# Fetching the sums of a graph's nodes group by group, before the last slot is stored

## The chip, the cores and the metric

The kernel runs on one core of a Trainium2 chip. The metric is the device time of one execution in microseconds. Three executions of the kernel before took 3168.97, 3172.85 and 3183.3 us; their median is 3172.85 us. A change is told by the median of the new kernel beside that of the old one.

## The reference

There are 6250 nodes with 64 features and 200,000 edges, sorted by their target node `dst`. Two graph networks follow each other:

```python
h = relu(layernorm(x))
# network 0: three layers of log-sum-exp over the neighbours
h = h @ W_in.T + b_in
for l in range(3):
    agg = log(segment_sum(exp(h[src]), dst))
    h = 0.5 * h + 0.5 * relu(layernorm(concat(h, agg) @ W_l[l].T + b_l[l]))
x = x + h
# network 1: a message per edge, summed per node, then a gated update
m = silu(silu(concat(x[src], sh, radial) @ W1 + b1) @ W2 + b2) @ W3 + b3
agg = segment_sum(m, dst)
u_in = concat(x, agg)
gate = sigmoid(u_in @ G + gb)
u = silu(layernorm(u_in @ U1 + ub1))
out = x + gate * layernorm(u @ U2 + ub2)
```

The sum over edges is linear in `W3` and `b3`, so the kernel sums first and multiplies by `W3` afterwards; the bias then comes in as `b3` times the node's number of edges (its degree).

## The kernel before

The nodes lie in J = 49 columns of 128. The kernel has these stages.

**Setup and counts.** VectorE makes two masks over the edges and SP stores them in device memory (L428 to L432). A flag (`way_known`) then chooses a way; with these inputs it is `by_counts`. There TensorE makes, from one-hot matrices, a matrix of edge counts between nodes, one block per column (L810), and multiplies it at once by the first layer's exponentials (L791). ScalarE copies each block out of PSUM in eleven pieces (`fill_block`, L1194) into one of two buffers, and SP stores the block (L474). `fill_block` of block j waits until block j - 2 is stored. Layers 2 and 3 read the blocks back. At the end of the counting `last_edges` computes, for each node, the row of its last edge (`end_idx`), in a dozen small operations on 128x49 elements.

**Messages.** The edges are cut into 391 slots of 512 (NSLOT). For each slot GpSimd gathers the rows of the source nodes with four indirect DMAs of 128 rows (L663), into a ring of 15 slots; every fifteenth slot is picked by matrix products instead (L961). TensorE transposes the rows (L950), multiplies by W1 (L973) and W2 (L980), with ScalarE's silu after each. VectorE scans along the slot (L2118) with a mask that restarts the sum at each new target node, so the scan at a node's last edge holds its whole sum. Four slots later TensorE multiplies the scan by W3 (`rows_back`, L988) into one PSUM bank, ScalarE copies it out (`rows_out`, L1342), and SP stores it as 512 rows of 64 numbers into `scan_rows` in device memory (`store_rows_of`, L550; in `sp.dma_start(scan_rows[bass.ds(s * BE, BE), :]...)`). One further row of `scan_rows`, number NO_EDGES, is zero and stands for nodes without edges. Five output buffers (OUT_RING) are used in turn, so that `rows_out` of slot s waits until slot s - 5 is stored.

**The end.** GpSimd waits until all slots are stored, and then fetches for each of the 49 columns the rows of its nodes' last edges with an indirect DMA that adds to `ybuf` (L678). `ybuf` holds b3 times the degree from a product on VectorE (L2131). The columns are in nine groups (END_GROUPS: seven of 6, one of 4 and one of 3). TensorE first multiplies 32 and then 8 filler products (`keep_busy`, L1027), whose results nobody reads. For each group: TensorE transposes the sums (`turn_agg`, L1037), ScalarE copies them (L1401), TensorE multiplies by U1 and G (`update_in`, L1049), VectorE adds the bias (L2153), ScalarE squares, VectorE reduces (L2176), ScalarE takes the root (L1388), VectorE scales (L2192), TensorE transposes (L1059), ScalarE applies silu (L1409), TensorE multiplies by U2 (`update_out`, L1068), and VectorE adds, normalises (L2198 to L2200) and applies the gate (`let_through`, L2206). GpSimd adds the result to x (L683) and SP stores it (L578). All engines run this as a pipeline, in which group i's first half stands beside the second halves of groups i - 1 to i - 3; the order is written out by hand and each engine keeps it.

**What sets the order.** Each engine works through its own list, with semaphores between. SP queues the mask stores, then the count blocks, then the loads and stores of the slots and of the output, all on one queue. GpSimd issues only the indirect DMAs and, at the end, the residual additions. `turn_done` counts the turned slots plus 15, so GpSimd's wait for `LOOP * i + k + 1` holds until the ring's slot is free.

Of the kernel before, what the change touches and what calls it, by code (L numbers as in the profile page):

```python
# [8 lines left out]
I32 = mybir.dt.int32  # L9
# [6 lines left out]
P = 128  # L16
# [23 lines left out]
LAG = 4  # L40
IDX_STEP = 5
# [71 lines left out]
def build(nc, x_in, dst_in, prev_in, first_in, src_in, src_row, rows_in, attr_in, w_in, v_in, out):  # L113
    with ExitStack() as ctx:
# [33 lines left out]
        end_idx = sb("end_idx", [P, J], I32)  # L148
# [109 lines left out]
        m_back = [ps[:, 2 + TERM_RING, k * TB * D:(k + 1) * TB * D] for k in range(BACK_RING)]  # L258

# [138 lines left out]
        update_ready, hT_stored, hT_loaded, let_in = (sem(n) for n in ("update_ready", "hT_stored", "hT_loaded", "let_in"))  # L398
# [15 lines left out]
        def _(sp):  # L414
# [17 lines left out]
            sp.wait_ge(masks_stored, 6 * DMA)  # L432

# [130 lines left out]

            for k in range(LOOP):
                move_slot(k, k)
# [7 lines left out]
            for s in range(NSLOT - LAG, NSLOT):  # L574
                store_rows_of(s, s % OUT_RING)
            for i, (a, n) in enumerate(END_GROUPS):
# [6 lines left out]
        def _(pool):  # L583
# [90 lines left out]
            for k in range(OUT_RING):  # L674
                pool.wait_ge(e1.stored[k], DMA * ((NSLOT - k + OUT_RING - 1) // OUT_RING))
            for i, (a, n) in enumerate(END_GROUPS):
                for j in range(a, a + n):
                    pool.indirect_dma_start(ybuf[:, j, :], None, scan_rows,  # L678
                                            bass.IndirectOffsetOnAxis(ap=end_idx[:, j:j + 1].bitcast(U32), axis=0),
                                            compute_op=ALU.add).then_inc(rows_fetched[i], DMA)  # L680
            for i, (a, n) in enumerate(END_GROUPS):
                pool.wait_ge(let_in, i + 1)
                pool.tensor_tensor(xres[:, a:a + n, :], xres[:, a:a + n, :], ybuf[:, a:a + n, :], ALU.add).then_inc(y_ready, 1)  # L683
# [3 lines left out]
        def _(pe):  # L687
# [294 lines left out]
            def rows_back(s, k, late):  # L982

                pe.wait_ge(e1.scan_done, s + 1)
                if late:
                    pe.wait_ge(e1.out_ready, s - BACK_RING + 1)
                for t in range(TB):
                    last = pe.matmul(m_back[k % BACK_RING][:, t * D:(t + 1) * D], m_scan[:, k % SCAN_RING, t * P:(t + 1) * P], W("W3"),  # L988
# [30 lines left out]
            for s in range(NSLOT - LAG, NSLOT):  # L1019
                rows_back(s, s % LOOP, True)  # L1020
# [8 lines left out]
            def turn_agg(i, a, n):  # L1029
# [5 lines left out]
                pe.wait_ge(rows_fetched[i], FETCHED + n * DMA)  # L1035
# [35 lines left out]
            keep_busy(6, 32)  # L1071
# [14 lines left out]
        def _(act):  # L1086
# [250 lines left out]
            def rows_out(s, k, lap):  # L1337
# [946 lines left out]
```

## Time and profile before

| | |
|---|---|
| median of three executions | 3172.85 us |
| profiled execution | 3195.68 us, span 3194.0 us |
| mean granted TensorE clock | 0.925 |
| TensorE, products / weight loads | 86% / 68% |
| VectorE | 60% |
| ScalarE | 51% |
| GpSimd | 47% |

Shares are of the span. The profile was taken from one execution; its time stands beside its span because what comes from the profile has to be put on its time. A busy TensorE is not TensorE at its peak, and a group's mean duration mixes both of its clock levels. In the lines of the profile L663 is line 663 of the kernel, PE is TensorE, DVE VectorE, ACT ScalarE, POOL GpSimd and SPq SyncE's queue of DMA issues. "Issue" is time in which the engine waited for nothing that the profile shows.

### The profile page before, as it was taken

How to read it: one execution, taken by the hardware profiler on the slowest of the kernel's cores; microseconds unless marked ns; L12 is line 12 of the kernel's file. 1: busy time of each engine (PE TensorE's matmuls, PEld its weight loads, DVE VectorE, ACT ScalarE, POOL GpSimd, SP SyncE). 2: the span in 40 equal slices, each digit the busy share in tenths (PEclk: the TensorE clock that was granted, in tenths of full speed). 3: DMA queues.
4: the chain of work that ended last, by engine and by line, in shares of the span. 5: the costliest groups of instructions: out<-in, count | busy, mean ns of one | idle time of the engine just before them, and what ended most of it. 6: DMA issues, size and time to landing. Idle time of an engine off the chain costs nothing.

```text
span 3194.0 us, 63519 instructions
## 1 busy us (share of the span) xinstructions
PE 2752.0 (86%) x20761; PEld 2179.8 (68%) x20761; DVE 1919.2 (60%) x2346; ACT 1613.8 (51%) x2994; POOL 1515.6 (47%) x1572
## 2 busy tenths in 40 slices
PE   4499999967999985889888989888989898898975
PEld 3377777757998982666666666666767666676654
DVE  5899999964444564455555555555555555555526
ACT  2488888832332223455545555545555554555534
POOL 4000000000000006777777777777777777777765
PEclk9999999968999996899999999999999999999976
DMA  3133333326998973445444445544445555444421
GB/s 109 61 141 161 141 161 141 161 121 260 365 361 320 359 287 79 107 121 132 120 119 119 122 117 125 129 121 121 121 117 125 119 128 124 120 121 116 126 48 30
DMA packets 216659, 477.09 MB, mean 149 GB/s; under 512 B 53932, under 2 KB 114910, under 8 KB 197601
## 3 DMA queue, kind: packets, MB, share of 16 engines
q1 hardware_dynamic: 159976, 422.33, 38.5%
q0 software_dynamic: 55632, 52.47, 10.3%
q10 hardware_dynamic: 1001, 1.66, 0.1%
q8 instruction: 28, 0.46, 0.1%
q14 instruction: 22, 0.18, 0.0%
HBM read 339.87 MB, written 136.41 MB: 149 GB/s over the span
## 4 chain that ended last, share of the span: by engine, by line
PE 47%; POOL 25%; issue 11%; DVE 11%; DMA 4%; ACT 1%; DVEq 0%; POOLq 0%; ACTq 0%
POOL arena L663 22%; PE ps L791 14%; PE ps L961 8%; PE ps L810 6%; PE ps L973 5%; PE ps L980 5%; PE ps L988 5%; DMA arena<-m_tab,m_idx 3%; DVE arena L1868 2%; POOL ybuf L678 2%; PE ps L950 2%; DVE stageT L1844 2%; PE ps L706 1%; PE ps L694 1%; POOL arena L604 0%
## 5 line engine op out<-in xcount | busy, mean ns | idle before, releaser
L663 POOL DMA_INDIRECT arena<-m_tab,m_idx x1463 | 1391.4, 951 | 1586.0 <-issue 1574.8
L2118 DVE TENSOR_TENSOR_SCAN arena<-arena,ps 128x512 f32<-128x512 f32 x391 | 500.2, 1279 | 856.6 <-ACT ps L1335 723.4
L988 PEld LDWEIGHTS ps<-weights,arena 128*128 128x128 f32 x3128 | 438.2, 203 | 210.3 <-issue 196.4
L1330 ACT ACTIVATE arena<-ps,weights 128x512 f32<-128x512 f32 x391 | 268.7, 687 | 490.7 <-PE ps L973 483.1
L791 PE MATMUL ps<-arena 128*128 128x195 bf16 (+1 forms) x4802 | 481.5, 248 | 32.2 <-DVE arena L1810 31.6
L791 PEld LDWEIGHTS ps<-arena 128*128 128x128 f16 x4802 | 416.8, 98 | 62.8 <-DVE arena L1810 31.8
L961 PE MATMUL ps<-ends,arena 128*128 128x192 bf16 x4900 | 458.9, 252 | 0.0
L973 PE MATMUL ps<-arena,weights 81*128 81x512 f32 x782 | 443.5, 651 | 0.0
L980 PE MATMUL ps<-arena,weights 128*128 128x512 f32 x782 | 435.9, 640 | 0.0
L961 PEld LDWEIGHTS ps<-ends,arena 128*128 128x128 bf16 x4900 | 421.7, 100 | 7.0
L988 PE MATMUL ps<-weights,arena 128*128 128x64 f32 x3128 | 415.4, 279 | 1.7 <-ACT arena L1342 1.7
L1323 ACT ACTIVATE arena<-ps 64x256 f32<-64x256 f32 x782 | 293.9, 376 | 218.5 <-PE ps L950 210.9
L1194 ACT ACTIVATE arena<-ps 128x588 f16<-128x588 f32 (+1 forms) x539 | 346.7, 644 | 107.0 <-PE ps L810 97.5
L2099 DVE TENSOR_SCALAR arena<-stage,node_no 128x3096 bf16<-128x3096 int16 (+1 forms) x225 | 368.9, 1640 | 0.0
L1868 DVE TENSOR_TENSOR arena<-arena 128x2352 bf16<-128x2352 f16 (+1 forms) x294 | 351.3, 1223 | 16.6 <-PE ps L810 16.6
L950 PE MATMUL ps<-ident,arena 128*128 128x128 f32 x782 | 165.5, 296 | 207.8 <-DMA arena<-m_tab,m_idx 204.6
L1335 ACT ACTIVATE ps<-ps,weights 128x512 f32<-128x512 f32 x391 | 258.8, 662 | 96.8 <-PE ps L980 93.5
L980 PEld LDWEIGHTS ps<-arena,weights 128*128 128x128 f32 x782 | 160.1, 205 | 207.9 <-issue 207.2
L950 PEld LDWEIGHTS ps<-ident,arena 128*128 128x128 f32 x782 | 97.2, 167 | 228.1 <-issue 224.9
L810 PE MATMUL ps<-arena 128*128 128x294 bf16 x1078 | 192.8, 298 | 34.2 <-DVE arena L1868 30.8
L791 PE MATMUL ps<-wide,arena 128*128 128x192 bf16 x2401 | 204.8, 247 | 6.4 <-DMA arena<-count_d 3.6
L791 PEld LDWEIGHTS ps<-wide,arena 128*128 128x128 f16 x2401 | 200.7, 99 | 7.2 <-issue 3.7
(269 smaller groups left out, 2294.1 us busy)
## 6 DMA issues: line engine op xcount, KB each, us to landing
arena<-count_d SPq DMA_DIRECT2D x98, 1568.0 KB, 8.5
arena<-keep_d SPq DMA_DIRECT2D x391, 256.0 KB, 3.9
count_d<-arena SPq DMA_DIRECT2D x49, 1568.0 KB, 5.1
scan_rows<-arena SPq DMA_DIRECT2D x391, 128.0 KB
arena<-m_tab,m_idx POOLq DMA_INDIRECT x1463, 3.3
arena<-attr_in SPq DMA_DIRECT2D x391, 34.0 KB
arena<-src_row SPq DMA_DIRECT2D x25, 258.0 KB
hT_d<-stageT ACTq DMA_DIRECT2D x12, 132.0 KB
```

Of the source, the lines that this page charges most:

```text
L663: pool.indirect_dma_start(m_rows[:, k, t, :], None, m_tab, bass.IndirectOffsetOnAxis(ap=m_idx[:, k, t:t + 1].bitcast(U32), axis=0))\
L791: last = pe.matmul(ps[:, bank, 0:rhs.shape[2]], blocks[block][:, a, :], rhs[:, a, :], start=(a == 0), stop=(a == J - 1), skip_group_check= ...
L810: last = pe.matmul(ps[:, bank, 0:WCOLS], hot_b[b][:, k % BATCH, :, i], hot_a[:, slot, k % UNIT, :, i], start=(i == 0), stop=(i == WT - 1))
L950: last = pe.transpose(m_turn[:, t // 2 * P:(t // 2 + 1) * P], m_rows[:, k, t:t + 2, :].rearrange("p t f -> p (t f)"), ident[:, :])
L961: last = pe.matmul(ps[:, 3 + TERM_RING + t // 2, (t % 2) * PARTS * D:(t % 2 + 1) * PARTS * D], pick[:, n % PICK_RING, (a - first) * PICK_C ...
L973: pe.matmul(m_in, W("W1"), m_msg[:, k % ATTR_RING, :], start=True, stop=True).then_inc(e1.in_done, 1)
L980: pe.matmul(m_term[k % TERM_RING], W("W2"), m_hid[:, k % HID_RING, :], start=True, stop=True).then_inc(e1.w2_done, 1)
L988: last = pe.matmul(m_back[k % BACK_RING][:, t * D:(t + 1) * D], m_scan[:, k % SCAN_RING, t * P:(t + 1) * P], W("W3"), start=True, stop=True)
L1194: act.activation(blocks[r][:, :, 2 * m * WD:2 * m * WD + 2 * wd].rearrange("p a (w d) -> p a w d", w=2), ps[:, two:two + 2, 0:wd * J].rear ...
L1868: dve.tensor_tensor(hot_a[:, u % HOT_SLOTS, 0:n, :, :], iota_w[:, :, :].unsqueeze(1).to_broadcast([P, n, WCOLS, WT]), keys, ALU.is_equal). ...
L2099: dve.tensor_scalar(of, src, node_no[:, first:first + 1], None, ALU.is_equal).then_inc(pick_ready, 1)
L2118: dve.tensor_tensor_scan(m_scan[:, k % SCAN_RING, :], m_mask[:, k % MASK_RING, :], m_term[k % TERM_RING], before, ALU.mult, ALU.add).then_ ...
```

## The change

1. The fetches at the end are plain ones instead of adding ones. Those of a group are issued as soon as the slots up to its last node's last edge are stored. VectorE computes that number for every node (`slots_needed`, four more operations in `last_edges`), GpSimd loads it into a register and waits for `out_ready` to reach it plus 5. After the last store SP adds 5 to `out_ready`, so that the last group's wait can end. A wait for `turn_done` keeps the semaphores of the gathers, which the fetches share, apart.
2. b3 times the degree goes to `hbuf` on VectorE, and VectorE adds it to each group's sums (`add_b3`), for group i + 1 ahead of group i's bias. TensorE waits for that.
3. VectorE adds the result to x, in place of GpSimd.
4. The last four slots' W3 products go to three PSUM banks in turn (`last_back`); the filler products move from bank 6 to bank 0.
5. SP stores zeros into the last 20 slots' rows of `scan_rows` (CLEARED), behind the masks, from the 64 zeros in one partition, and waits for it ahead of the first slot.

```diff
+CLEARED = LOOP + OUT_RING
+        last_back = [ps[:, 2 + TERM_RING + k % 3, 0:TB * D] for k in range(LAG)]
 @@ SP
             sp.wait_ge(masks_stored, 6 * DMA)
+            sp.dma_start(scan_rows[(NSLOT - CLEARED) * BE:NSLOT * BE, :], zero_row[:, :].unsqueeze(1).to_broadcast([1, CLEARED * BE, D]))\
+              .then_inc(zero_stored, DMA)
...
+            sp.wait_ge(zero_stored, 2 * DMA)
             for k in range(LOOP):
                 move_slot(k, k)
...
+            for k in range(OUT_RING):
+                sp.wait_ge(e1.stored[k], DMA * ((NSLOT - k + OUT_RING - 1) // OUT_RING))
+            sp.sem_inc(e1.out_ready, OUT_RING)
 @@ GpSimd
-            for k in range(OUT_RING):
-                pool.wait_ge(e1.stored[k], DMA * ((NSLOT - k + OUT_RING - 1) // OUT_RING))
             for i, (a, n) in enumerate(END_GROUPS):
+                needed = slots_needed[P - 1:P, a + n - 1:a + n]
+                pool.wait_ge(e1.turn_done, LOOP * (LAPS - 1) + i + 2)
+                pool.wait_ge(e1.out_ready, pool.to_reg(pool.value_load(needed, min_val=OUT_RING + 1, max_val=NSLOT + OUT_RING)))
+                pool.sem_inc(alone, 1)
                 for j in range(a, a + n):
                     pool.indirect_dma_start(ybuf[:, j, :], None, scan_rows,
-                                            bass.IndirectOffsetOnAxis(ap=end_idx[:, j:j + 1].bitcast(U32), axis=0),
-                                            compute_op=ALU.add).then_inc(rows_fetched[i], DMA)
-            for i, (a, n) in enumerate(END_GROUPS):
-                pool.wait_ge(let_in, i + 1)
-                pool.tensor_tensor(xres[:, a:a + n, :], xres[:, a:a + n, :], ybuf[:, a:a + n, :], ALU.add).then_inc(y_ready, 1)
+                                            bass.IndirectOffsetOnAxis(ap=end_idx[:, j:j + 1].bitcast(U32), axis=0))\
+                        .then_inc(rows_fetched[i], DMA)
 @@ TensorE
-            def rows_back(s, k, late):
+            def rows_back(s, k, late, to=m_back[0], ring=BACK_RING):
                 pe.wait_ge(e1.scan_done, s + 1)
                 if late:
-                    pe.wait_ge(e1.out_ready, s - BACK_RING + 1)
+                    pe.wait_ge(e1.out_ready, s - ring + 1)
...
-            for s in range(NSLOT - LAG, NSLOT):
-                rows_back(s, s % LOOP, True)
+            for n, s in enumerate(range(NSLOT - LAG, NSLOT)):
+                rows_back(s, s % LOOP, True, last_back[n], n + 1 if n < 3 else 3)
...
-                pe.wait_ge(rows_fetched[i], FETCHED + n * DMA)
+                pe.wait_ge(agg_ready, i + 1)
...
-            keep_busy(6, 32)
+            keep_busy(0, 32)
 @@ VectorE, last_edges
+                link(dve.tensor_scalar(mean[:, :], end_f[:, :], BE - 1.0, float(BE), ALU.add, ALU.max))
+                link(dve.tensor_copy(slots_needed[:, :], mean[:, :]))
+                link(dve.tensor_scalar(slots_needed[:, :], slots_needed[:, :], BE.bit_length() - 1, None, ALU.logical_shift_right))
+                link(dve.tensor_scalar(slots_needed[:, :], slots_needed[:, :], OUT_RING, None, ALU.add))
 @@ VectorE, the end
-                    link(dve.tensor_tensor(ybuf[:, :, :], per_node(deg_one[:, :, 0], D), per_feature(V("b3"), J), ALU.mult))
+                    link(dve.tensor_tensor(hbuf[:, :, :], per_node(deg_one[:, :, 0], D), per_feature(V("b3"), J), ALU.mult))
...
+            def add_b3(i, a, n):
+                dve.wait_ge(rows_fetched[i], FETCHED + n * DMA)
+                dve.tensor_tensor(ybuf[:, a:a + n, :], ybuf[:, a:a + n, :], hbuf[:, a:a + n, :], ALU.add).then_inc(agg_ready, 1)
...
-                dve.scalar_tensor_tensor(v, of_rows[:, a:a + n, HID:ROW], 1.0, v, ALU.add, ALU.mult).then_inc(let_in, 1)
+                link(dve.scalar_tensor_tensor(v, of_rows[:, a:a + n, HID:ROW], 1.0, v, ALU.add, ALU.mult))
+                dve.tensor_tensor(xres[:, a:a + n, :], xres[:, a:a + n, :], v, ALU.add).then_inc(y_ready, 1)
             for i, (a, n) in enumerate(END_GROUPS):
                 v = i - 2 if i >= 2 else None
+                if i == 0:
+                    add_b3(i, a, n)
+                if i + 1 < len(END_GROUPS):
+                    add_b3(i + 1, *END_GROUPS[i + 1])
                 add_update_bias(i, a, n)
```

ScalarE's `rows_out` reads the bank that `rows_back` wrote.

## Rows read from the trace of the kernel before

**Rows 1.** The page's chain that ended last, share of the span by line.

```profile
POOL arena L663 22%; PE ps L791 14%; PE ps L961 8%; PE ps L810 6%; PE ps L973 5%; PE ps L980 5%; PE ps L988 5%; DMA arena<-m_tab,m_idx 3%; DVE arena L1868 2%; POOL ybuf L678 2%; PE ps L950 2%; DVE stageT L1844 2%; PE ps L706 1%; PE ps L694 1%; POOL arena L604 0%
```

**Rows 2.** One line's instructions: count, duration in ns min/median/max, first and last start.

```profile
L663 POOL DMA_INDIRECT arena<-m_tab,m_idx x1463: 940/945/4143, 1207.0 to 3043.0; - x183
...
L678 POOL DMA_INDIRECT ybuf<-scan_rows,end_idx x49: 1531/1541/1936, 3063.7 to 3153.9; - x49
```

**Rows 3.** Timeline (start us, us, engine, line, operation, count), end of the message pass.

```profile
3042.99 0.95 POOL L663 DMA_INDIRECT arena<-m_tab,m_idx  x1 [0.30 <-issue]
...
3053.84 2.69 DVE L2118 TENSOR_TENSOR_SCAN arena<-arena,ps 128x512 f32<-128x512 f32 x2 [1.39 <-ACT ps L1335]
3053.94 1.00 PE L988 MATMUL ps<-weights,arena 128*128 128x64 f32 x8
...
3057.14 1.72 PE L988 MATMUL ps<-weights,arena 128*128 128x64 f32 x8 [0.57 <-ACT arena L1342]
...
3059.43 1.94 PE L988 MATMUL ps<-weights,arena 128*128 128x64 f32 x8 [0.56 <-ACT arena L1342]
...
3061.16 6.03 PE L1027 MATMUL ps<-ones 128*128 128x256 bf16 x40
...
3063.75 1.58 POOL L678 DMA_INDIRECT ybuf<-scan_rows,end_idx  x1 [19.81 <-DMA scan_rows<-arena]
```

**Rows 4.** Timeline of the end: groups 0 and 8, one group's products and transposes.

```profile
3077.74 0.80 ACT L1401 ACTIVATE wide<-ps 64x768 f32<-64x768 f32 x1 [15.95 <-PE ps L1037]
...
3078.69 4.18 PE L1049 MATMUL ps<-weights,wide 128*128 128x192 f32 x12 [0.98 <-ACT wide L1401]
...
3082.91 1.36 DVE L2153 TENSOR_TENSOR arena<-ps,rowvec 128x1152 f32<-128x1152 f32 x1 [26.37 <-PE ps L1049]
...
3098.79 1.46 PE L1037 MATMUL ps<-ident,ybuf 128*64 128x128 f32 x6 [4.36 <-DMA ybuf<-scan_rows,end_idx]
...
3122.35 2.66 PE L1068 MATMUL ps<-weights,stageT 128*128 128x64 f32 x12
...
3170.85 0.54 DVE L2153 TENSOR_TENSOR arena<-ps,rowvec 128x384 f32<-128x384 f32 x1
...
3185.85 0.59 POOL L683 TENSOR_TENSOR xres<-xres,ybuf 128x192 f32<-128x192 f32 x1 [1.47 <-DVE ybuf L2206]
```

**Rows 5.** Windows: start:end, length, busy us per engine, TensorE clock, DMA share, GB/s.

```profile
3070.00:3080.00 10.00, 2.80 (x10) 2.23 (x11) 0.00 (x0) 0.80 (x1) 8.48 (x6) 0.55 0.20 17
3106.03:3114.94 8.91, 4.72 (x36) 4.22 (x34) 4.99 (x9) 5.87 (x9) 7.39 (x6) 1.00 0.21 18
3129.00:3139.86 10.86, 8.19 (x38) 7.78 (x37) 7.23 (x13) 6.33 (x9) 9.23 (x6) 0.68 0.21 18
```

**Rows 6.** Timeline of VectorE at the end: an addition, and a small operation beside L683.

```profile
3116.79 0.56 DVE L2199 TENSOR_TENSOR ybuf<-ybuf,rowvec 128x384 f32<-128x384 f32 x1
...
3155.60 3.15 DVE L2172 TENSOR_SCALAR mean<-mean 128x6 f32<-128x6 f32 x1
```

**Rows 7.** Timeline: one operation on 128x49 in the last edges.

```profile
669.24 0.19 DVE L1636 TENSOR_SCALAR end_f<-end_f 128x49 f32<-128x49 f32 x1
```

**Rows 8.** Windows of the kernel's start, around the mask stores.

```profile
82.00:84.00 2.00, 0.19 (x1) 0.20 (x2) 1.83 (x7) 0.00 (x0) 0.00 (x0) 1.00 1.06 440
85.00:143.40 58.40, 19.77 (x88) 12.30 (x89) 51.47 (x77) 24.78 (x41) 0.00 (x0) 1.00 0.00 1
```

**Rows 9.** First count blocks: DMA issues, SP's timeline, ScalarE's timeline.

```profile
count_d<-arena SPq DMA_DIRECT2D x49, 1568.0 KB, 5.1
...
143.45 43.67 SPq L474 DMA_DIRECT2D count_d<-arena  x5
...
154.25 1.96 ACT L1194 ACTIVATE arena<-ps 128x392 f16<-128x392 f32 x3 [0.39 <-PE ps L810]
```

**Rows 10.** The page's DMA queues: packets, MB, share of 16 engines.

```profile
q1 hardware_dynamic: 159976, 422.33, 38.5%
q0 software_dynamic: 55632, 52.47, 10.3%
```

More of the change, by code:

```diff
@@ L147, in build @@
             "mean", "var", "rstd", "end_tile", "end_f", "start_f", "has", "degree"))
-        end_idx = sb("end_idx", [P, J], I32)
+        end_idx, slots_needed = sb("end_idx", [P, J], I32), sb("slots_needed", [P, J], I32)
         stage = sb("stage", [P, 2, GT, P])
@@ L397, in late_block @@
             return first % RING, first // RING + k + 1, first + RING * k
-        update_ready, hT_stored, hT_loaded, let_in = (sem(n) for n in ("update_ready", "hT_stored", "hT_loaded", "let_in"))
+        update_ready, hT_stored, hT_loaded, agg_ready = (sem(n) for n in ("update_ready", "hT_stored", "hT_loaded", "agg_ready"))
         agg_turned, agg_copied, agg_multiplied = (sem(n) for n in ("agg_turned", "agg_copied", "agg_multiplied"))
@@ L980, in hidden_out @@
                 pe.matmul(m_term[k % TERM_RING], W("W2"), m_hid[:, k % HID_RING, :], start=True, stop=True).then_inc(e1.w2_done, 1)
-            def rows_back(s, k, late):
+            def rows_back(s, k, late, to=m_back[0], ring=BACK_RING):
                 pe.wait_ge(e1.scan_done, s + 1)
                 if late:
-                    pe.wait_ge(e1.out_ready, s - BACK_RING + 1)
+                    pe.wait_ge(e1.out_ready, s - ring + 1)
                 for t in range(TB):
-                    last = pe.matmul(m_back[k % BACK_RING][:, t * D:(t + 1) * D], m_scan[:, k % SCAN_RING, t * P:(t + 1) * P], W("W3"),
+                    last = pe.matmul(to[:, t * D:(t + 1) * D], m_scan[:, k % SCAN_RING, t * P:(t + 1) * P], W("W3"),
                                      start=True, stop=True)
@@ L1335, in second_silu, with rows_out @@
                 act.activation(m_term[k % TERM_RING], m_term[k % TERM_RING], ACT.Silu, bias=W("b2")).then_inc(e1.silu2_done, 1)
-            def rows_out(s, k, lap):
+            def rows_out(s, k, lap, of=m_back[0]):
                 act.wait_ge(e1.back_done, s + 1)
@@ L1341, in rows_out @@
                     act.wait_ge(e1.stored[k % OUT_RING], DMA * ((LOOP // OUT_RING) * lap + k // OUT_RING))
-                act.activation(m_out[:, k % OUT_RING, :, :].rearrange("p t f -> p (t f)"), m_back[k % BACK_RING], ACT.Copy)\
+                act.activation(m_out[:, k % OUT_RING, :, :].rearrange("p t f -> p (t f)"), of, ACT.Copy)\
                    .then_inc(e1.out_ready, 1)
@@ L1368, in _ @@
                 second_silu(s, s % LOOP)
-            for s in range(NSLOT - LAG, NSLOT):
-                rows_out(s, s % LOOP, s // LOOP)
+            for n, s in enumerate(range(NSLOT - LAG, NSLOT)):
+                rows_out(s, s % LOOP, s // LOOP, last_back[n])
             def square_u(i, a, n):
```

## The prediction

> **What bounds the kernel now.** I read the chain of waits first, by line, and then in order of time. Its shares [rows 1] name two stretches that the change touches: the gathers of the message pass (L663) and the fetches at the end (L678). From 3000 us on, the chain is GpSimd's gathers, one after another, 1.25 us apart (0.95 us and 0.30 us of issue [rows 3]). The last gather is issued at 3043.0 [rows 2], so GpSimd reaches the end of its loop at 3044 and not fifteen slots early. It then waits 19.8 us for the last stored slot and issues 49 fetches, 1.84 us apart, from 3063.75 to 3155.5 [rows 2, 3].
>
> The timeline of the end shows the update of the nodes running in step with the fetches: VectorE adds the update bias (L2153) to group 0 at 3082.91, to group 8 at 3170.85 [rows 4]. A full group takes 10.9 us, as long as its six fetches (6 x 1.84 = 11.0). In that time VectorE is busy for 7.2 us and TensorE for 8.2 [rows 5]. The fetches are the bound, and after them the chain VectorE, ScalarE, TensorE. The profiled execution took 3195.68 us with a span of 3194.0, some 23 us above the median of 3172.85. I work out differences in the span and put them on the median.
>
> **The end, part by part.** *The last W3 products.* Four slots' products run from 3053.94 to 3061.37 [rows 3], each after the first waiting for ScalarE's copy out of the one bank (idle 0.57 us), the last two at a fallen clock (1.72 and 1.94 us instead of 1.00). With three banks only the scans hold them. The last two scans end at 3055.1 and 3056.5, so slot 390's product ends near 3058.3. That is 3 us gained.
>
> *The fetches.* A plain fetch has the shape of the gathers (128 rows of 256 B), so I price it like them at 1.25 us from one to the next. Bounds: 1.25 and 1.84, the accumulating form. GpSimd starts at 3044.3, since the turns that it now waits for (slots 377 to 385) are over by then, and so are the stores that groups 0 to 7 need (group 7 ends near slot 368: 5888 nodes x 32 edges / 512). Each group adds a register load and three waits, for which no row stands; 0 to 1 us each, I take 0.5. Group 0 is then in at 3044.3 + 8.0 + 3.3 = 3055.6, group 1 at 3064, group 8 (3 columns, after the last store at about 3061) at 3044.3 + 61 + 5 + 3.3 = 3114. The old wait of 19.8 us and the fetches no longer bound anything; late next is the chain of the updates.
>
> *The start.* TensorE goes from 3058.3 into its 40 filler products, now on the path. They took 6.0 us when they hid in the wait [rows 3]; at the full clock, which unbroken work should hold, some 4.5. Then transposes 0.8 to 1.5, copy 0.8, the products of group 0 2.1 to 4.2 (the rows' 1.46 and 4.18 are at the low level, and half of it at full clock) [rows 4] and 0.6 of hand-over: the first L2153 comes at 3068 (3067 to 3071) instead of 3082.91.
>
> *The groups.* VectorE's 7.23 us in a full group [rows 5] grow by adding b3 times degree and by the residual add, each a 128x384 float32 addition like L2199, 0.56 us [rows 6]: 8.35 of work. With the waits for square and square root between them I get 8.9. From the other side, TensorE at its low level needs 4.18 for L1049, 1.46 for each of two sets of transposes and 2.66 for L1068 [rows 4], 9.8 us per group and 10.1 with waits. The clock was 0.68 in one old group and 1.00 in another [rows 5], so I take 9.4. GpSimd's residual adds go, and with them stalls such as VectorE's 3.15 us at L2172, an operation on 128x6 elements, while L683 ran [rows 6]. From group 0 to 8: 8.7 + 6 x 9.4 + 7.8 = 72.9, so group 8's L2153 comes at 3141 instead of 3170.85. From there to the end were 23.15 us. VectorE's own adds replace GpSimd's 0.59 us last one [rows 4], but those of groups 5 to 7 stand ahead of it: 23.5.
>
> The end: 3141 + 23.5 = 3164.5, against 3194.0: 29.5 us gained. Bounds: 34 (periods of 8.9) and 20 (periods of 10.1, a late start, fetches at 1.84, by which group 8 would be in at 3044.3 + 90 + 5 + 3 = 3142, about 5 us late).
>
> **The start of the kernel.** Four small operations on 128x49 join the chain of the last edges, 0.19 us and the hand-over each [rows 7]: 0.9 us lost, on VectorE's path. The b3 product (3.4 us) is the same into another buffer.
>
> *The clearing transfer.* SP queues one store of 20 x 512 = 10,240 rows of 256 B, 2.62 MB, all read from one row of one partition. It starts when the masks have landed: the transfer engines stand from 85 on [rows 8], so the first bytes move at about 86. Up to 143.45 the DMA engines have nothing else to do [rows 8]. That is the cover, and it is limited: at 143.45 SP queues the first count block (1568 KB, 5.1 us to landing) on the same queue [rows 9], and ScalarE may fill the third block, whose buffer is that of the first, only when this one has landed. ScalarE begins it at 155.0, right behind the second (L1194, [rows 9]). So a clearing of up to 155.0 - 5.1 - 86 = 64 us is free. Every further microsecond delays the count stage, which is on the chain itself (L791 is 14% of it, L810 6% [rows 1]).
>
> No row shows a large store out of one partition; the other rows that bear on it spread over 128 partitions or go from HBM. From below: at 440 GB/s [rows 8] it takes 6 us, no loss. By the mean time of SP's packets, 38.5% x 16 x 3194 / 159,976 = 0.123 us [rows 10], 640 on each of 16 engines take 79 us. That is 15 us too long. By one partition's share: 440 GB/s over 16 engines is 27.5 GB/s for each, each with eight partitions of its own; if all sixteen must draw on one partition and get no more than one of them had, 2.62 MB take 95 us. From above: if rows out of one partition went one after another at an engine's own time for such rows (10.3% x 16 x 3194 us for some 197,000 rows [rows 2, 10] = 26.7 ns), 273 us.
>
> I take 95 us, since reading from a single partition is what sets this store apart. It ends at 181, the first count block lands at 186.4, and ScalarE waits from 155.0: 31.4 us. TensorE can work some 2 us ahead into its free banks. Against that, its clock will have fallen while it stood: after the idle 3063 to 3076 it read 0.55 from 3070 to 3080 [rows 5]. I leave the loss at 31.5.
>
> The Trainium skill (SBUF — State Buffer, "Door 1: the DMA port swizzle") says that four neighbouring partitions share one of 16 ports and reached 27.6 GB/s together. By it the clearing would take 95 us, and this trace has no such store to set against it. Another rule speaks against the change more strongly (DMA: Bandwidth & Descriptors, "Why small descriptors are slow"): a 256 B descriptor pays 3 cycles on top of 8. If that held at the port too, my estimate from these pages is 131 us, and the kernel would lose some 38 us net.
>
> **Sum.** -29.5 at the end, +0.9 in the last edges, +31.5 in the count stage: +3 us. On the median: 3176 us, no change. About 0.5% (16 us) is what a measurement of this kernel can tell from none.
>
> **Rivals.** *The clearing hides (faster).* If it is over in 64 us, only the gain is left: 3172.85 - 29.5 + 0.9 = 3144 us. For it speaks that 57 us of idle transfer engines lie ahead of the first block [rows 8]; against it that 2.62 MB come from one partition. Clearing by packets (79 us) would lie between: +13, 3157. Chance of a result under 3157: 0.30.
>
> *The clearing is slower than one engine's share (slower).* The sixteen engines' reads of one partition would get in each other's way. The place is the same wait of ScalarE for the third block. It decides from a clearing of 111 us on, where the net loss passes 16 us. At 273 us the wait would be 209 us: 3172.85 - 28.6 + 209 = 3353. Against it: no packet in the trace comes near such a cost; for it: no row excludes it. Chance of over 3189: 0.20.
>
> *The end gains less.* If a plain fetch also costs 1.84 us, or TensorE stays at its low level, the gain is 20 to 24 us. With the clearing at 95 us the time is 3182 to 3186, still no change; it only shifts within the cases. That the fetches don't start early at all would need GpSimd's new wait to hold until the last store at 3061; then 49 x 1.25 start there, group 0 is in at 3072 and the end gains about 13 us: 3192. One in twenty, inside the 0.20.
>
> **Numbers.** No change 0.50, faster 0.30, slower 0.20. The forecast is 3176; its own range 3166 to 3188. The range for 8 in 10 goes from 3139 (clearing hidden, periods short) to 3212 (a clearing 36 us longer than forecast), which cuts the slower case in half.
>
> **What would show it.** The clearing's time to landing, 95 us. L1194 idle for some 31 us before the third block near 155, and every later stage up to the last gather later by about 32 us. The last L988 product to the first L2153: 10 us. L2153 of full groups 8.9 to 10.1 us apart; L678 at 0.95 us; no POOL L683. I am wrong if the clearing lands before 150 (then faster), or if the L678 lines still run past 3120 of the old time scale.

## The result, and the profile after

The changed kernel takes 3170.1 us (median of 20 runs) against 3184.7 for the kernel before in the same rounds: a ratio of 0.9954 [0.9936, 0.9972], 14.6 us faster. The forecast was +3 us, no change. The forecast's base, 3172.85 us, was the median of three executions; the 20 give 3184.7. The executions of each kernel fall into two clusters, at 3171.0 and 3191.9 us before and at 3156.0 and 3170.9 after (their medians, with the executions taken beside a0; 15.0 and 21.0 us apart), and every trace of either kernel is of an upper one. The profiled pair has spans of 3194.0 and 3169.4 us; it stands 24.6 us apart, more than the medians.

Most of it is two large terms of opposite sign, and a smaller one that the change did not aim at. First the start, in windows of the kernel after (columns as in [rows 8]):

```profile
100.00:120.00 20.00, 1.49 (x5) 1.11 (x5) 13.31 (x21) 0.00 (x0) 0.00 (x0) 1.00 0.10 27
160.00:180.00 20.00, 3.98 (x35) 2.81 (x32) 5.81 (x5) 1.64 (x3) 0.00 (x0) 0.65 0.10 28
180.00:200.00 20.00, 10.57 (x81) 8.31 (x81) 6.49 (x7) 8.38 (x15) 0.00 (x0) 0.67 0.41 167
```

The clearing store moves 27 GB/s from 86 us on and is over near 183 us. SP's and ScalarE's timelines, and the chain of waits (start, us, what), show whom that holds up:

```profile
85.34 0.67 SPq L435 DMA_DIRECT2D scan_rows<-zero_row  x1
150.95 28.40 SPq L478 DMA_DIRECT2D count_d<-arena  x1
```
```profile
188.66 1.77 ACT L1201 ACTIVATE arena<-ps 128x588 f16<-128x588 f32 x3 [26.34 <-SPq L481]
```
```profile
150.95 37.49 DMA count_d<-arena
```

The first count block, queued at 150.95, lands 37.5 us later instead of 5.1, behind the clearing. ScalarE's third block begins at 188.66 instead of 155.0 [rows 9]: 33.7 us lost. The last count block is stored 34.6 us later (688.4 against 653.8), and the four operations in the last edges cost 0.9 us more: TensorE's first product after the counting (L701, L694 before) comes 19.8 us behind the last block's store instead of 18.9.

The layer update that follows then gives back 8.8 us. These are 32 us of it, from 18 us behind the last block's store on, in the kernel before, in the changed kernel and in e7, a run below:

```profile
671.80:703.80 32.00, 30.95 (x147) 30.80 (x147) 18.56 (x33) 7.70 (x8) 0.00 (x0) 0.50 0.13 53
```
```profile
706.40:738.40 32.00, 18.89 (x147) 18.35 (x147) 26.24 (x42) 9.24 (x10) 0.00 (x0) 0.82 0.12 52
```
```profile
715.40:747.40 32.00, 30.23 (x145) 30.26 (x146) 19.26 (x35) 7.70 (x8) 0.00 (x0) 0.50 0.12 52
```

TensorE had almost nothing to do for 14 to 15 us ahead of all three, and its granted clock had fallen to 0.50 (1.2 GHz). In the changed kernel it is back at 1.00 (2.4 GHz) 24 us behind the last block's store. In the kernel before it stays low: 147 products take 30.95 us instead of 18.89, and they hold up the layer. This is no scatter of one pair. The stretch from the last block's store to the first gather takes 553.2 to 553.6 us, at 0.50, in the traces of the kernel before, b1, b2 and e7, and 545 to 547 us, at 0.82, in the other 16. The first three of the four have at most the clearing of the change, but e7 has all of it and lacks only the filler products of the end. So what decides the level is open.

The end, in the timeline of the kernel after: fetches, last W3 products, fillers, and the first and the ninth addition of the update's bias (L2169, which was L2153).

```profile
3069.82 0.94 POOL L688 DMA_INDIRECT ybuf<-scan_rows,end_idx  x1 [0.30 <-issue]
...
3081.43 3.76 PE L995 MATMUL ps<-weights,arena 128*128 128x64 f32 x32
...
3085.02 4.53 PE L1034 MATMUL ps<-ones 128*128 128x256 bf16 x40
...
3091.19 2.19 PE L1056 MATMUL ps<-weights,wide 128*128 128x192 f32 x12 [0.98 <-ACT wide L1408]
...
3093.42 1.36 DVE L2169 TENSOR_TENSOR arena<-ps,rowvec 128x1152 f32<-128x1152 f32 x1 [6.73 <-PE ps L1056]
...
3151.99 0.55 DVE L2169 TENSOR_TENSOR arena<-ps,rowvec 128x384 f32<-128x384 f32 x1
...
3166.95 0.36 DVE L2223 TENSOR_TENSOR xres<-xres,ybuf 128x192 f32<-128x192 f32 x1
```

The fetches begin 1.25 us after the last gather, 15 us ahead of the end of the last W3 product, and never hold an update but one (1.66 us before L2163 of group 1). From the end of the last W3 product (3085.2) to the first bias addition there are 8.2 us instead of 21.5; from there to the ninth 58.6 instead of 87.9; from there to the end of the span 17.4 instead of 23.2 [rows 4]. With 1.8 us in the last W3 products (16.6 instead of 18.4 us after the last gather) the end gains 50.2 us. 35.5 lost and 50.2 gained give -14.7. The rest of the pair's -24.6 us is 8.3 in the counted layers (the 8.8, less 0.5 behind them) and 1.6 in the gathers. So that -14.7 meets the medians' -14.6 is in part luck: the two terms explain 14.7 of the 24.6 us of the only pair that was traced.

Windows of the kernel after, the whole end and two full groups in it:

```profile
3085.20:3167.30 82.10, 55.29 (x342) 49.06 (x340) 65.88 (x135) 55.64 (x83) 36.58 (x37) 0.83 0.14 38
3121.43:3129.51 8.08, 8.08 (x38) 7.49 (x37) 7.80 (x16) 6.22 (x9) 6.25 (x7) 0.58 0.20 49
3129.51:3137.45 7.94, 4.99 (x37) 4.47 (x36) 7.67 (x16) 6.22 (x9) 2.63 (x3) 1.00 0.16 41
```

In the last line VectorE is busy for 7.67 of 7.94 us, and TensorE, at a clock of 1.00, for 4.99. In the group of the second line the clock was 0.58 and TensorE was busy for all of its 8.08 us, and it took no longer than the one before it, which had the full clock (8.07). That is the reading to take against [rows 5]: the bound has moved from the fetches to VectorE, and TensorE has room, or at its low level just keeps up.

### The profile page after: what moved, and what is told of

Same layout as the page of the kernel before. It is cut to its first block, busy times and chain, and to the rows that moved or that the text cites. A ratio compares the mean times of both kernels' runs of the same rounds, so it can differ in the third digit from the quotient of the medians.

```text
span 3169.4 us, 63570 instructions
## 1 busy us (share of the span) xinstructions
PE 2721.7 (86%) x20761; PEld 2151.2 (68%) x20761; DVE 1922.3 (61%) x2368; ACT 1612.1 (51%) x2994; POOL 1476.7 (47%) x1563
## 3 DMA queue, kind: packets, MB, share of 16 engines
q10 hardware_dynamic: 1001, 1.66, 0.1%
## 4 chain that ended last, share of the span: by engine, by line
PE 39%; POOL 29%; issue 13%; DVE 12%; DMA 5%; ACT 2%; DVEq 1%; POOLq 0%; ACTq 0%; SPq 0%
POOL arena L671 29%; PE ps L798 14%; PE ps L817 6%; PE ps L968 6%; PE ps L980 3%; PE ps L987 3%; PE ps L995 3%; DMA arena<-m_tab,m_idx 3%; DVE arena L1879 2%; DVE stageT L1855 1%; PE ps L957 1%; DMA count_d<-arena 1%; PE ps L713 1%; PE ps L701 0%; POOL arena L612 0%
```

## The experiments

The result above, a0, b1, e1 and e2 ran where the message pass takes some 1830 us. All other runs ran on chips (0, 7, 12 and 14) where it takes some 3000 us and the kernel before 4374 to 4437 us. The count stage is as long there as elsewhere, but absolute times do not compare. So each ratio is taken to the kernel before on the same chip in the same rounds, and beside it I compare stretches whose operations have the same durations.

**The changed kernel again (a0), five rounds.**

> The changed kernel once more, as the yardstick for the others. Theory (the clearing store costs some 34 us in the count stage and the end gains some 50): its profile shows again ScalarE's first piece of the third count block (L1201) near 188.7 us, and 84 us from the last W3 product to the end; 0.995 of the kernel before. Rival (the first profile was a lucky execution): the stretch between the count stage and the last gather differs by several us from the first profile, and the ratio with it.

Measured 3169.46 us, 0.9954 [0.9928, 0.9979], the same stages to within 1 us (the first bias addition comes 0.9 us sooner).

**The clearing alone (b1)**: the kernel before with the one store.

```diff
+            sp.dma_start(scan_rows[(NSLOT - CLEARED) * BE:NSLOT * BE, :], zero_row[:, :].unsqueeze(1).to_broadcast([1, CLEARED * BE, D]))\
+              .then_inc(zero_stored, DMA)
...
+            sp.wait_ge(zero_stored, 2 * DMA)
             for k in range(LOOP):
```

> The kernel before with nothing but the clearing store added. Theory: it moves at 27 GB/s, ends near 183 us, holds back the first count block's store, and ScalarE waits some 26 us for the third block's buffer, which begins 33 to 34 us later; every later stage follows: 3184.7 + 34 = 3218 us, 1.0105 of before. Rival (the loss in the profile of the changed kernel is made up later, or comes from other parts of the change): at most 15 us, 1.005.

Measured 3242.83 us, 1.0171 [1.0136, 1.0206], 56 us slower, over 20 us more than the share of the changed kernel's clearing; its last count block is stored 51.2 us late. A window of b1, and its wait (us in total, times, longest):

```profile
100.00:110.00 10.00, 0.47 (x1) 0.18 (x1) 9.26 (x5) 0.00 (x0) 0.00 (x0) 1.00 0.51 24
```
```profile
ACT arena L1198 <- SPq L480: 45.7, 1, 45.7
```

The store runs at 24 GB/s and not 27, and the DMA engines' share is 0.51 instead of 0.10. One thing that differs is where the zeros lie: at byte 139,552 of the partition here, 32 bytes past a multiple of 256, and at 139,776, a multiple, in the changed kernel. So:

**The clearing alone, aligned (b2)**: b1 with 224 bytes ahead of zero_row.

```diff
+        pad = sb("pad", [P, 56])
         zero_row = sb("zero_row", [1, D])
```

> The kernel before with the clearing store, as in b1_clear_alone, and one unused tile of 224 bytes ahead of zero_row, which moves zero_row from byte 139552 to 139776 of its partition, a multiple of 256, where the changed kernel has it. Theory (a row that does not start at a multiple of 256 bytes takes one beat more of the partition's door, 9 instead of 8; the Trainium skill, DMA: Bandwidth & Descriptors, How a descriptor splits into AXI transactions): 27.5 GB/s instead of 24, the store over near 183 us instead of 198, the count stage 34 to 35 us late instead of 51: about 3221 us, 1.011 of before. Rival (the kernel before is slowed by something else than the place of the zeros): 24 GB/s and 3240 us again.

Measured 1.0087 [1.0056, 1.0118] (on chip 0), and in the same stretch of b2:

```profile
100.00:120.00 20.00, 5.99 (x24) 3.91 (x22) 17.59 (x26) 3.42 (x10) 0.00 (x0) 1.00 0.10 27
```

Alignment alone brings the rate back to 27 GB/s. The last count block is stored at 697.4, where the changed kernel's variants e3 and e4 have 696.3 and 695.8 on the same chip, and 662 where the zeros come out of 16 partitions (e9, e10): so the aligned clearing, and nothing else of the change, delays the count stage. The Trainium skill (DMA: Bandwidth & Descriptors, "How a descriptor splits into AXI transactions") says that a read which starts off a multiple of 256 B is begun at the multiple below and pays beats of 32 B for bytes it doesn't use. By it a shifted 256 B row costs nine beats instead of eight, by my estimate 27.5 x 8 / 9 = 24.4 GB/s; the trace has 24. Why the DMA share reads 0.51 then, no run shows.

**Zeros out of 128 and of 16 partitions (e1, e2)**: the changed kernel with

```diff
-        zero_row = sb("zero_row", [1, D])
+        zero_row = sb("zero_row", [P, D])
...
-            sp.dma_start(scan_rows[(NSLOT - CLEARED) * BE:NSLOT * BE, :], zero_row[:, :].unsqueeze(1).to_broadcast([1, CLEARED * BE, D]))\
+            sp.dma_start(scan_rows[(NSLOT - CLEARED) * BE:NSLOT * BE, :].rearrange("(p t) f -> p t f", p=128),
+                         zero_row[0:128, :].unsqueeze(1).to_broadcast([128, CLEARED * BE // 128, D]))\
```

(e2: 16 for 128.)

> The changed kernel, with the same 2.62 MB of zeros read from 128 partitions instead of one. Theory: the 97 us were the one partition's share; over 128 partitions the store moves at 200 to 440 GB/s and is over in 6 to 16 us, no wait for the block's buffer, third block near 155, 34 us gained: 3136 us, 0.985 of before. VectorE's stall of 8.1 us ahead of the count stage goes too. Rival (256 B writes into device memory are what is slow): still 60 us or more, so a part of the loss or all of it stays.

> The same zeros read from the first 16 partitions. Theory of the Trainium skill (SBUF - State Buffer, Door 1: the DMA port swizzle): 16 neighbouring partitions lie on 4 ports, so the store moves at about 4 x 27 = 109 GB/s and takes 24 us. Rival (each partition by itself can give 27 GB/s): 16 x 27 = over 400 GB/s, 6 us. Both are over by 143 us, so the time is that of the kernel with 128 partitions; the GB/s in the windows from 86 us on tell them apart.

Measured 3136.33 us, 0.9841 [0.9811, 0.9872], and 3134.03 us, 0.9838 [0.9799, 0.9877]. The same window of e1 and of e2:

```profile
87.00:95.00 8.00, 5.41 (x23) 3.71 (x24) 7.44 (x22) 3.64 (x11) 0.00 (x0) 1.00 1.27 290
```
```profile
87.00:95.00 8.00, 5.42 (x23) 3.72 (x24) 7.45 (x22) 3.54 (x11) 0.00 (x0) 1.00 0.37 102
```

The clearing is over within 10 and 25 us, the first count block is queued at 143.5 again and the last at 654.0, as before. Both kernels beat both given ones; they differ by less than their intervals. What the clearing costs is the difference to a0, 33 to 35 us. The rates tell two readings apart: one partition gives 27 GB/s, 16 partitions 102, 128 partitions 290, so 16 partitions do not give sixteen times 27. By the rule of the Trainium skill that the prediction drew on (SBUF — State Buffer, "Door 1: The DMA port swizzle"), four neighbouring partitions share a port of 27.6 GB/s: one port for the single row and four for 16 partitions, which I estimate at 4 x 27.6 = 110 GB/s. The traces agree (27 and 102). At 128 partitions something else is the limit, and no run shows what.

**Fetches held back until everything is stored (e3)**: the changed kernel with

```diff
+            pool.wait_ge(e1.out_ready, NSLOT + OUT_RING)
             for i, (a, n) in enumerate(END_GROUPS):
                 needed = slots_needed[P - 1:P, a + n - 1:a + n]
```

> The changed kernel, with GpSimd waiting for the last stored slot before its first fetch. It starts some 2.4 us after the last W3 product instead of 15 us ahead of it; group 1, which VectorE adds b3 to ahead of group 0's bias, is in 21 us after the last product instead of 1. Theory (the early start is worth the wait for groups 0 and 1, and after them VectorE is slower than the fetches): the first L2169 comes 22 us after the last product instead of 8, the distances of the groups stay at 7.9 us: +14 us, 3184 us. Rival (the early start is worth the whole gain of the end, since the fetches would bound the groups again): +25 us or more, groups 8.5 us or more apart.

> The changed kernel, but GpSimd fetches only when all rows of the message pass are stored. In two runs with the message pass of 3000 us the first update bias came 21 us after the last W3 product instead of 8.5, and ScalarE then stood still for 36 us. Theory 1 (where the message pass takes 1830 us, that stop is gone and late fetches cost the shift alone): +13 to +14 us. Theory 2 (the stop comes from late fetches as such): groups 0 to 8 106 us instead of 59, +55 to +60 us.

Three runs, on chips 0, 12 and 0: 1.0104, 1.0104 and 1.0089. In each the first update bias comes 21 us after the last W3 product, as expected, and then ScalarE stands still. Its timeline in the third:

```profile
4376.14 0.80 ACT L1409 ACTIVATE wide<-ps 64x768 f32<-64x768 f32 x1 [18.30 <-remote]
4407.68 0.99 ACT L1417 ACTIVATE stageT<-ps,weights 128x768 f32<-128x768 f32 x1 [27.50 <-remote]
```

The last fetch is issued at 4399.9, and after it the groups run at their usual pace; groups 0 to 8 take 106 us instead of 59. The stop lasts while the fetches run back to back, and the section on the slower chips takes it up. Neither theory is decided: what a late start costs where there is no such stop was not measured.

**Adding fetches (e5)**: the changed kernel with the one old form put back.

```diff
                     pool.indirect_dma_start(ybuf[:, j, :], None, scan_rows,
-                                            bass.IndirectOffsetOnAxis(ap=end_idx[:, j:j + 1].bitcast(U32), axis=0))\
-                        .then_inc(rows_fetched[i], DMA)
+                                            bass.IndirectOffsetOnAxis(ap=end_idx[:, j:j + 1].bitcast(U32), axis=0),
+                                            compute_op=ALU.add).then_inc(rows_fetched[i], DMA)
...
-                dve.tensor_tensor(ybuf[:, a:a + n, :], ybuf[:, a:a + n, :], hbuf[:, a:a + n, :], ALU.add).then_inc(agg_ready, 1)
+                dve.sem_inc(agg_ready, 1)
```

> The changed kernel, with the fetches adding to b3 times degree in ybuf, as before, but issued early; VectorE's addition of b3 goes. Theory (the fetches took 1.84 us each because they add, and at that price they would be the bound even when they start early): 49 x 1.84 = 90 us from 15 us ahead of the last product on, group 8 in 79 us after it, where VectorE needs it 60 us after it: groups 11 us apart, +16 to +19 us, 3187 us. Rival (the early start alone does it): within 5 us of the changed kernel.

> The changed kernel with fetches that add into a ybuf preset to bias times degree. Where the message pass took 3000 us instead of 1830, they started 49 us ahead of the last W3 product and their 90 us were hidden (last product to last update's bias 65.5 us). Here they have 14 us ahead. Theory 1 (1.84 us per adding fetch paces the end): groups 10.8 us apart, +15 to +19 us over the changed kernel. Theory 2: within 5 us.

Four runs, on chips 0, 12, 0 and 7: 0.9976, 0.9961, 0.9950, 0.9956 [0.9939, 0.9972], the only one of the variants without a repaired clearing that is faster than before there. Its fetches take 90 us, but they begin 49 us before the last W3 product, and the 22 of the 49 that are left after it stay ahead of VectorE: groups 0 to 8 take 57.0 us. No run of it was made where the message pass takes 1830 us, so the price of an adding fetch there, with a head start of 15 us, is open.

**One bank for the last products (e6)**

```diff
-        last_back = [ps[:, 2 + TERM_RING + k % 3, 0:TB * D] for k in range(LAG)]
+        last_back = [ps[:, 2 + TERM_RING, 0:TB * D] for k in range(LAG)]
...
-                rows_back(s, s % LOOP, True, last_back[n], n + 1 if n < 3 else 3)
+                rows_back(s, s % LOOP, True, last_back[n], 1)
```

> The changed kernel with the last four W3 products in one PSUM bank, one after another behind ScalarE's copy. Theory 1: the last product ends 2.5 to 3.4 us later and all of the end moves with it: +2.5 to +3.4 us. Theory 2: the first group's sums, and not the last product, are awaited, and the products of the last slots are off the path: under 1 us.

Measured 1.0093 [1.0067, 1.0119]. From the start of the last scan to that of the last product there are 5.9 us, against 2.2 in the changed kernel: 3.7 us for the three banks. In the total no run shows them, since the changed kernel has no run on that chip. PE's timeline of e6 shows the waits for ScalarE's copy and the fallen clock of [rows 3] back again:

```profile
4386.90 1.94 PE L995 MATMUL ps<-weights,arena 128*128 128x64 f32 x8 [0.56 <-ACT arena L1349]
4389.41 1.94 PE L995 MATMUL ps<-weights,arena 128*128 128x64 f32 x8 [0.57 <-ACT arena L1349]
```

**No filler products (e7)**: the changed kernel without the 32 fillers ahead of the first group and the 8 beside each of groups 0 and 1.

```diff
-                if i < 2:
-                    keep_busy(3, 8)
...
-            keep_busy(0, 32)
```

> The changed kernel without the 40 filler products ahead of the first group and the 2 x 11 beside groups 0 and 1 (they compute nothing that is used). Theory 1 (they keep TensorE's clock up, and the clock is what lets the groups come 7.3 us apart instead of my 9.4): the end runs at a granted clock near 0.5 instead of 0.83, groups 9 to 10 us apart, first update bias 4 us sooner: +10 to +15 us over the changed kernel. Theory 2 (VectorE's own work sets the distance, and my 9.4 was too long because I let TensorE's low level set it): groups stay 6.5 to 7.9 us apart, and the 4.5 us of fillers come off: -4 to -3 us.

Measured 1.0075 [1.0054, 1.0095]. A window of its end:

```profile
4402.00:4477.00 75.00, 48.14 (x270) 42.19 (x270) 63.81 (x133) 53.58 (x80) 0.32 (x1) 0.77 0.06 23
```

The clock is 0.77 here, not near 0.5. From group 0 to 8 it is 0.86, against 0.88 in the changed kernel, and they take 59.9 us, against 58.6 there, 59.3 in a0 and 60.0 in e2. All of that difference lies in the last distance, from group 7 (four columns) to group 8, where VectorE has less to do: it is 6.6 to 6.7 us where the clock is 0.95 or more and 8.05 where it is 0.50 (e7, e2 and one e4). From the last scan to the end of the span there are 84.0 us, against 86.7 in the changed kernel's profile and 87.9 in a0's. Theory 2 holds: VectorE's work sets the distance, and the fillers on the path cost the end some 3 to 4 us. Leaving them out is not shown to be a gain in all: e7 is the one variant of the changed kernel whose first layer update ran at 0.50, some 8 us longer.

**Residual additions on GpSimd (e4: all nine; e9: six of nine, with zeros out of 16 partitions)**

```diff
-                link(dve.scalar_tensor_tensor(v, of_rows[:, a:a + n, HID:ROW], 1.0, v, ALU.add, ALU.mult))
-                dve.tensor_tensor(xres[:, a:a + n, :], xres[:, a:a + n, :], v, ALU.add).then_inc(y_ready, 1)
+                dve.scalar_tensor_tensor(v, of_rows[:, a:a + n, HID:ROW], 1.0, v, ALU.add, ALU.mult).then_inc(let_in, 1)
...
+            for i, (a, n) in enumerate(END_GROUPS):
+                pool.wait_ge(let_in, i + 1)
+                pool.tensor_tensor(xres[:, a:a + n, :], xres[:, a:a + n, :], ybuf[:, a:a + n, :], ALU.add).then_inc(y_ready, 1)
```

> The changed kernel, with the addition to x on GpSimd again. Theory (GpSimd's drain after its last computing instruction, 7.9 us in the kernel before, held the end): from the last addition to the end of the span 7.6 us again instead of 2.1; VectorE has 0.56 us less in each group, but small VectorE operations beside GpSimd's additions take up to 3 us. Together 0 to +6 us: 3170 to 3176 us. Rival (the additions cost VectorE as much as they cost GpSimd, the drain is no matter): -4 us.

> A version that should beat both: zeros out of 16 partitions, and the residual additions of groups 0 to 5 on GpSimd, those of groups 6 to 8 on VectorE, so that GpSimd's closing drain of some 8 us runs beside the last two groups. Theory 1 (VectorE paces the groups): 0.56 us less in each of six groups, 2 to 4 us under the kernel with zeros from 16 partitions (0.9838 of before): 0.9830 to 0.9820. Theory 2 (the two engines get in each other's way, as VectorE's 3.15 us at L2172 did): equal or up to 3 us slower.

Measured: e4 1.0120 and 1.0103, e9 1.0010 [0.9999, 1.0021]; e2 has no run on e9's chip, so e9's two theories are told apart by its trace alone. In e4 the last addition starts 9.7 us before the end of the span, in the changed kernel 2.5. GpSimd's closing drain in the kernel before, in e4 and in the changed kernel, each with SP's branch behind the last store (count: duration in ns, start):

```profile
L114 POOLq DRAIN  x1: 7907/7907/7907, 3185.8 to 3185.8; - x1
L114 SPq COMPARE_BRANCH  x1: 38/38/38, 3188.1 to 3188.1; - x1
```
```profile
L115 POOLq DRAIN  x1: 9545/9545/9545, 4465.4 to 4465.4; - x1
L115 SPq COMPARE_BRANCH  x1: 38/38/38, 4467.6 to 4467.6; - x1
```
```profile
L115 POOLq DRAIN  x1: 25042/25042/25042, 3116.6 to 3116.6; - x1
L115 SPq COMPARE_BRANCH  x1: 38/38/38, 3169.0 to 3169.0; - x1
```

With the addition on GpSimd as the last operation its drain ends 5.6 us (before) and 7.4 us (e4) behind SP's branch, and the span ends with it. In the changed kernel GpSimd has a drain too, and a long one, but it ends at 3141.6, 9 us behind its last fetch and long before the last store. So the drain does not go away; it runs beside VectorE's last groups. And the additions taken from VectorE give nothing back: groups 0 to 8 take 59.8 and 58.6 us in the two runs of e4 and 58.4 in e9, against 58.6 to 60.0 in the changed kernel and its variants above. The timelines of GpSimd and of VectorE in e9 say why:

```profile
4402.46 0.99 POOL L698 TENSOR_TENSOR xres<-xres,ybuf 128x384 f32<-128x384 f32 x1 [7.05 <-DVE ybuf L2231]
```
```profile
4402.74 1.53 DVE L2216 TENSOR_TENSOR stage<-arena,rstd 128x768 f32<-128x768 f32 x1
```

L2216 takes 0.96 us when GpSimd is idle and 1.53 beside its addition: 0.57 lost for 0.56 saved. The Trainium skill (SBUF — State Buffer, "Who interferes with whom") says that a VectorE instruction with two inputs in SBUF contends with a GpSimd instruction that reads SBUF. The trace agrees, and it looks like a plain wait: 4402.46 + 0.99 + 0.96 is 4404.4, and L2216 ends at 4404.3.

**What plain fetches do on the slower chips.** In e4, e6, e7 and e9, with plain fetches from the last gather on, the last slots of the message pass take 103 to 107 us after it. In e5 and e10, with adding fetches, they take 50, and in e3, where the same plain fetches are held back, 50 too. PE's timeline of e7 beside the fetches:

```profile
4322.97 0.32 PE L968 MATMUL ps<-ends,arena 128*128 128x192 bf16 x1 [2.48 <-issue]
4325.07 0.32 PE L968 MATMUL ps<-ends,arena 128*128 128x192 bf16 x1 [1.78 <-issue]
4327.87 0.32 PE L968 MATMUL ps<-ends,arena 128*128 128x192 bf16 x1 [2.48 <-issue]
```
```profile
4343.30 0.69 ACT L1334 ACTIVATE arena<-ps,weights 128x512 f32<-128x512 f32 x1 [47.73 <-remote]
```

Products that follow one another without a gap elsewhere come singly, 2.1 to 2.8 us apart and with nothing to wait for that the profile knows, and ScalarE stands for 47.7 us. In e5, with its fetches 1.84 us apart, and in e3, with none yet, TensorE is busy for 49.0 of the same 49.0 us at a clock of 1.00. In e3 the stop comes later, beside the fetches, 47 us in the end. So on these chips it goes with the stretch in which plain fetches are issued, wherever that lies; it takes back some 50 us, all of the end's gain. The kernels with plain fetches and zeros out of one partition are 0.8 to 1.2% slower than before there. Whether the plain form or the closer pace (1.25 us instead of 1.84) brings the stop, no run tells. That the engines' instructions come late is my reading of "issue"; no run isolates it. The changed kernel itself has no run there, only variants that differ from it in few us of work.

**Both repairs (e10)**: zeros out of 16 partitions as in e2, adding fetches as in e5.

> The version that both kinds of chip point to: the changed kernel with zeros out of 16 partitions and with fetches that add into a ybuf preset to bias times degree. Where the message pass takes 3000 us: theory 1 (the two gains are independent: 34 us of clearing, and the stop of the other engines that plain fetches cause): 0.9956 - 34/4437 = 0.988 of before. Theory 2 (they overlap, as part of the clearing's delay is given back in the message pass): 0.992 to 0.995. Where it takes 1830 us: theory 1 (the price of an adding fetch paces the end): 0.9838 plus 15 to 19 us, 0.9885 to 0.990; theory 2 (it is hidden): 0.984.

Measured on chip 14: 4328.6 us against 4376.8, 0.9899 [0.9883, 0.9916]. 48 us are gained of the 52 that independent gains would give. The interval lies between the two theories and reaches neither. It is the only variant that beats the kernel before on the slower chips by 1%; it has no run where the message pass takes 1830 us, and there e1 and e2 are the best measured. No run leaves the clearing out altogether.

## Why the forecast was wrong, by its own steps

*The clearing: right.* The rate was taken as one engine's share, 27.5 GB/s; it is 27, so the store takes 97 us instead of 95 and ends near 183. The wait was forecast as 31.4 us and is 33.7, since the store ends 2 us later; by the last block it is 34.6. VectorE also lost 7.5 us ahead of the first block (below), but these lie inside the wait and cost nothing. The last edges cost 0.9, as forecast. b2 and e1 show that it is this store, and that it costs this. Two figures of the rivals don't follow from the sum: clearing by packets comes to 3159 us, not 3157, and 16 us are lost from a clearing of 109 us on, not 111. Neither matters for the result.

*The early fetches: right.* They start behind the last gather, at 1.25 us each, and the first L2153 was put 9.7 us after the last product; it came after 8.2. The three banks bring the last product from 5.7 us after the last scan to 2.2, 3.5 us for 3 forecast; but the last scan itself comes 14.1 us after the last gather instead of 12.3, so that 1.8 are left.

*The groups: here it failed.* "From the other side, TensorE at its low level needs ... 9.8 us per group ... so I take 9.4." From group 0 to 8 that made 72.9 us; measured were 58.6, 14.3 less. The step let TensorE at its low clock set the period. Over the groups its clock was 0.88 in the changed kernel, against 0.70 before, and it needs 5.0 to 5.1 us per full group at 1.00; where the clock fell to 0.58 the group still took 8.08 us. What sets the period is VectorE's work. [rows 5] held the number: in its group at 1.00 TensorE was busy for 4.72 us. That the waits for fetches were what lowered the clock fits these figures, but no run isolates it. VectorE's 8.35 us of work was too high as well, 7.67 to 7.80 measured: the old group's 7.23 [rows 5] held 0.27 of a stretched L2177, and its operations overlap by some hundredths each. And the first three distances are 6.5, 6.5 and 6.9 us, since the later parts of earlier groups do not lie in them yet. In e7 the full groups' distances are the same without fillers (7.93 and 7.87 us at clocks of 0.79 and 0.64, 7.94 and 7.88 in the changed kernel at 1.00 and 0.60). Only the last distance still hangs on the clock, by 1.4 us.

*What follows the last addition: missed.* The step kept 23.5 us from group 8 to the end; it took 17.4. GpSimd's closing drain, 7.9 us [its row above], stood in the trace of before between the last operation and the end of the span, 5.6 us of it behind the last store, and I priced only the 0.59 us of the addition. e4 brings it back.

*The layer update after the counting: no term.* The forecast moved every later stage by the delay of the count stage alone. In the profiled pair the counted layers also became 8.3 us shorter by TensorE's clock, and the gathers 1.6.

The end gained 14.3 + 6.1 + 1.5 - 1.2 = 20.7 us more than forecast, and the start cost 3.1 more: +2.9 becomes -14.7. The rival "the end gains less" pointed the wrong way; none had the end gain more. The two forecast terms nearly cancelled, so an error of 14 us in one of them was enough to turn the sign, although the clearing, the term that most of the rivals were about, was right.

## What to carry to other kernels

When the wait that starves an engine goes, don't price that engine at the clock it had while it starved: take its durations from a stretch where it was kept busy, and let the engine with the most work per round set the period. Look at what stands between a kernel's last operation and the end of its span, engine by engine. Compare the stages that a change does not touch over all traces before calling their difference scatter. A large fill should come from many partitions and from an address on a multiple of 256 bytes, and a variant that wins on one chip should be run on a second one.

## What the runs showed of the hardware

- A store that reads 256 B rows of one partition: 27 GB/s, 24 when the row lies 32 B off a multiple of 256; 102 from 16 partitions, 290 from 128.
- Beside such a store the five engines' register loads of `use_counts` from SBUF took 7.7 to 8.4 us each (VectorE's, L2062, 8104 ns); in the kernel before they took 0.47 to 0.55 (VectorE's 549 ns), and in e1 and e2 the same. That is the 7.5 us by which the first count block was queued later in the changed kernel.
- GpSimd's closing drain ended 7 to 9 us behind the end of its last operation in the kernel before, in e4 and in the changed kernel; it shows in the span only where GpSimd's work comes last.
- After the counting TensorE's granted clock came back to 1.00 some 24 us behind the last count block's store in 16 traces and stayed at 0.50 in 4, the same way in every trace of the same kernel, for a difference of 7 to 8 us. Why is open.
- Of the five chips on record (0, 6, 7, 12, 14) number 6 ran the message pass in 1830 us and the others in some 3000. Why was not found; no run was made for it.
